# Every product of the last stage with its columns in descending order

## What is computed

```
x = u
# block 1, on LN(x)
z       = rmsnorm(LN(x)) @ in_proj.T            # 768 channels, then a causal 3-tap convolution
x2,x1,v = split(z)
y       = (long_conv(x1*v, h) + x1*v*D) * x2    # h: sums of 16 exponentials per channel
y       = y @ out_proj.T + LN(x)                # out_projection
zm      = rmsnorm(y)
mlp     = gelu(zm @ l1.T) * (zm @ l2.T) @ l3.T  # mlp_block, mlp_down; hidden size 672
x       = x + LN(y + mlp)
# block 2, on LN(x)
W1', W2' = W1, W2 plus rank-one terms from 16 tokens of the batch
hid     = gelu(LN(x) @ W1'.T + b1)              # ffn_up, hidden size 1024
x       = x + LN(hid @ W2'.T + b2)              # ffn_down
```

## Time and profile before

| | us |
|---|---|
| median of 3 runs | 1077.68 |
| lowest, highest | 1077.45, 1081.7 |
| the profiled execution | 1076.75 |
| its span, first to last instruction | 1075.0 |
| TensorE busy in the span | 1050.8 |
| VectorE busy | 877.8 |
| ScalarE busy | 710.8 |
| mean granted TensorE clock | 1.000 |

### The profile page before, as it was taken

One profiled execution on the slowest core, in us unless ns is written; L12 is line 12 of the kernel. 1 busy time (PEld: TensorE's weight loads), 2 busy tenths in 40 slices (PEclk: granted clock), 3 DMA queues, 4 the chain that ended last, 5 costly groups with the idle time before them and its releaser, 6 DMA issues.

```text
span 1075.0 us, 24951 instructions
## 1 busy us (share of the span) xinstructions
PE 1050.8 (98%) x9012; PEld 1008.5 (94%) x9012; DVE 877.8 (82%) x2322; ACT 710.8 (66%) x1589; POOL 299.5 (28%) x575
## 2 busy tenths in 40 slices
PE   8899999999999999999999999999999999999998
PEld 7777888899989999999999999989999999999997
DVE  7999998774788888888887878897888888887776
ACT  7879887764456666666666666656666666666644
POOL 7677775470101112111111111111112111111111
PEclk9999999999999999999999999999999999999999
DMA  3337977986322222233222222432222223222000
GB/s 130 120 117 236 294 216 196 363 318 151 83 66 41 54 57 50 52 52 58 59 60 58 52 51 60 122 96 41 60 51 50 52 53 59 59 58 60 21 21 31
DMA packets 112491, 102.83 MB, mean 96 GB/s; under 512 B 7552, under 2 KB 103744, under 8 KB 112112
## 3 DMA queue, kind: packets, MB, share of 16 engines
q1 hardware_dynamic: 111136, 98.67, 36.2%
q0 software_dynamic: 736, 2.51, 0.6%
q10 hardware_dynamic: 496, 0.05, 0.0%
HBM read 75.75 MB, written 30.70 MB: 99 GB/s over the span
## 4 chain that ended last, share of the span: by engine, by line
PE 67%; DVE 6%; issue 2%; ACT 1%; POOL 0%; POOLq 0%; DVEq 0%; ACTq 0%
PE ps_ring L1551 35%; PE ps_w L1551 16%; PE ps_m L1551 9%; PE ps_o L1551 4%; PE ps_rt L1566 2%; DVE base L1373 1%; PE ps_w L1561 1%; DVE bn L1277 1%; PE ps_m L1617 1%; DVE prod L1320 0%; DVE ht_l L1289 0%; DVE pt_l L1289 0%; POOL sc L1129 0%; ACT rows L1254 0%; DVE yrow L1512 0%
## 5 line engine op out<-in xcount | busy, mean ns | idle before, releaser
L1129 POOL TENSOR_TENSOR sc<-sc,small 128x2 f32<-128x2 f32 x127 | 94.5, 744 | 676.8 <-DVE sc L1501 404.6
L1194 ACT ACTIVATE gate<-ps_ring 128x256 f32<-128x256 f32 x192 | 73.0, 381 | 129.7 <-PE ps_ring L1551 128.9
L1215 ACT ACTIVATE hid<-ps_ring,small 128x256 f32<-128x256 f32 x256 | 112.1, 483 | 24.2 <-PE ps_w L1551 13.4
L1551 PE MATMUL ps_ring<-mt_l,wl_h 128*128 128x256 f32 x640 | 125.5, 277 | 2.6 <-DVE mt_l L1289 2.6
L1551 PE MATMUL ps_ring<-mt_h,wl_h 128*128 128x256 f32 x640 | 125.5, 277 | 1.8 <-DVE prod L1320 1.3
L1551 PE MATMUL ps_ring<-mt_h,wl_l 128*128 128x256 f32 x640 | 124.9, 277 | 0.0
L1289 DVE TENSOR_TENSOR ht_l<-hid,ht_h 128x256 fp32r<-128x256 f32 x256 | 103.1, 423 | 16.5 <-ACT ht_h L1219 10.6
L1551 PE MATMUL ps_ring<-xt_h,we_h 128*128 128x256 f32 x512 | 104.8, 285 | 2.5 <-DVE prod L1320 2.4
L1551 PE MATMUL ps_ring<-xt_h,we_l 128*128 128x256 f32 x512 | 101.3, 279 | 0.0
L1551 PE MATMUL ps_ring<-xt_l,we_h 128*128 128x256 f32 x512 | 101.3, 279 | 0.0
L1320 DVE TENSOR_TENSOR prod<-ps_ring,gate 128x256 f32<-128x256 f32 x192 | 80.7, 420 | 24.2 <-ACT gate L1194 20.6
(11 more groups left out here) (203 smaller groups left out, 2720.2 us busy)
## 6 DMA issues: line engine op xcount, KB each, us to landing
toep_scratch<-taps_scratch SPq DMA_DIRECT2D x26, 512.0 KB, 7.4
toep<-toep_scratch SPq DMA_DIRECT2D x26, 512.0 KB, 8.8
xa<-in_x SPq DMA_DIRECT2D x16, 512.0 KB, 4.9
x_scratch<-x2c SPq DMA_DIRECT2D x16, 512.0 KB, 3.7
x2s<-x_scratch SPq DMA_DIRECT2D x32, 256.0 KB, 6.7
xa_c<-in_x SPq DMA_DIRECT2D x32, 256.0 KB, 2.7
xb_c<-in_x SPq DMA_DIRECT2D x32, 256.0 KB, 2.7
yin<-seq SPq DMA_DIRECT2D x124, 64.0 KB, 5.5
```

Source lines behind the costliest of these rows:

```text
L1129: nc.gpsimd.tensor_tensor(sc[:, to], sc[:, to], neg_half[:, 0, 0:CC], ALU.pow).then_inc(S[done], 1)
L1194: nc.scalar.activation(gate[rows_of, m % 2], ring[m % RING][rows_of, 0], ACT.Gelu_apprx_tanh).then_inc(S["gate_done"], 1)
L1215: nc.scalar.activation(hid[:, m % HIDS], block_of, ACT.Gelu, bias=b1s[:, m:m + 1]).then_inc(S["hid_done"], 1)
L1551: mm = nc.tensor.matmul(out, lhs(a, kk), rhs(b, kk), start=(j == 0), stop=(closed and j == len(todo) - 1))
```

## The change

One line in `product` changes. The last dimension of both the streamed operand and the output is walked from its last element to its first, with step -1. Column 255 of `rhs` goes in first and its result is written to column 255 of `out`, and so on down to column 0. Each result lands in the same element as before, with the same sum. The weights (`lhs`), the count of instructions, their order, the semaphores and every other line are as before. The matmuls at L1561, L1566 and L1617 keep their ascending order.

```
--- before.py
+++ after.py
@@ -1548,7 +1548,7 @@
                     if j == HIGHS_FIRST:
                         for there in highs_ready:
                             pe.wait_ge(*there)
-                    mm = nc.tensor.matmul(out, lhs(a, kk), rhs(b, kk), start=(j == 0),
+                    mm = nc.tensor.matmul(out[:, ::-1], lhs(a, kk), rhs(b, kk)[:, ::-1], start=(j == 0),
                                           stop=(closed and j == len(todo) - 1))
                 return mm
```

## The result

| | before | after |
|---|---|---|
| median, us | 1078.91 (4 runs) | 1101.95 (4 runs) |
| lowest, highest | 1077.45, 1081.7 | 1100.69, 1104.16 |
| ratio, 95% interval | | 1.0213, 1.0184 to 1.0241 |
| the profiled execution | 1076.75 | 1101.98 |
| its span | 1075.0 | 1100.2 |

A forecast was written before the change was run, and what follows sets the result against it. The prediction took the last stage to be bound by distances between matmul starts on a gapless TensorE. Its terms summed 0 + 0 + 0 + 0, giving a median of 1077.7 us, range 1070 to 1102.

The forecast's parts named there:

- rival 2: A small price per matmul, by address phase or the turn at L1617: 1083 to 1101 us, chance 0.20.
- The likeliest case: No change in time: 1077.7 us, own range 1075 to 1081, chance 0.53 within 0.5%.
- What bounds the kernel: Last stage: TensorE without slack, so each ns on the distance between 6528 matmul starts costs 6.5 us.
- Semaphores, weight loads, DMAs, the tail: Parts the change leaves alone, including VectorE, GpSimd and last DMA after the final matmul: 0 us.
- Reading downwards: Streamed operand read with step -1: taken as 0, from a backward VectorE read at the forward rate.
- 119.2 ns, the other end: Upper bound per matmul for reading downwards, if each column takes two slots.
- Writing PSUM downwards: Output written with step -1: taken as 0, bounds 0 or 119.2 ns a matmul, with less confidence.
- half rate: Each descending column takes its own slot, most likely in the PSUM write: 1847 to 1856 us; family's chance 0.20.
- one column in about 120: Share of columns delayed by a slot (0.83 ns of 113) at which the slow side already decides.
- The turn at L1617: 64 places where an add follows a write of the same element: taken as 0, at most 10.4 us.
- Start addresses: Streamed operand starts 1020 bytes further on, beside weight loads: taken as 0, bounds -7.1 to +23.0 us.
- Address phase: one kind of product alone moves: Sign for a price by start address: one product's distance changes, the other kinds keep theirs.

The follow-up runs named there:

- read_only: Step -1 on the streamed operand alone, output written upwards, against the kernel before: 1101.56 us against 1077.59, ratio 1.0226.
- write_only: Step -1 on the output alone, operand streamed upwards, against the kernel before: 1077.83 us, ratio 1.0005.
- down_weights: The change only in output projection, MLP down and second feed-forward product, which stream weight matrices, against the kernel before: 1093.92 us, ratio 1.0163.
- The blocks: Three runs of the kernel before with trains of equal, unread matmuls added at the end, varying operands and order; distances mostly 113.3 to 120.0 ns.
- turn_after: Kernel before, all ascending, with four transposes moved behind the first feed-forward product: 1082.44 us, ratio 1.0053.

## Why the prediction was right and where it wasn't

The range held the time, but by luck: 1101.95 us lies 0.05 under its end of 1102, and 0.95 above the 1083 to 1101 of rival 2, a small price per matmul, which is the case that came. The likeliest case, no change at 1077.7 us with a chance of 0.53, did not come.

- What bounds the kernel: right. From 330 to 560 us TensorE has no gap in either trace, and from 560 to 860 under 4 us of them, so each ns on the distance went straight to the end. 0.84 us more in a unit of 204 matmuls is 4.1 ns each, by 6.5 us per ns some 27 us; 25.2 came, as a few units gained less.
- Semaphores, weight loads, DMAs, the tail: right, 0. The pieces at L1566 and L1617 kept their lengths. (The duration of a matmul of the MLP, which was to stay near 276 ns, became 282.)
- Reading downwards, "I take 0": the step that failed. It took a VectorE row at 1.33 ns a column for a sign about a reader at 0.44 ns, which the text itself called no exclusion. `read_only` measured 24.0 us for it, 3.7 ns a matmul, and 119.2 ns, the other end, was over 30 times too far.
- Writing PSUM downwards, "I take 0": right; `write_only` measured 0.2 us. The half rate named as most likely for this path is shut out on both paths. (That it decides from one column in about 120 is a slip: by the text's own 0.83 of 113 ns it is one in about 136; nothing hangs on it.)
- The turn at L1617: right at 0. The piece is 0.12 us in both traces, where waiting for the drain would have made it 0.28.
- Start addresses: the bound of +23.0 us, made from the kernel's own two distances, was near the right size, and for a related reason: an access order that moves a train from one distance to a slower one. The text took it for a property of the operands ("differ by nothing but the operands"). That was wrong: the same operands stood at 113.3 and 117.8 ns in the kernel before itself, and the ascending MLP moved to 117.7 in `down_weights`. And its arithmetic let the first feed-forward product stay at 117.9 and the rest come up to it; in truth the token products went to 119.8, 1.9 ns above it, and the others to 118. The sum is also too high by its own rows: it takes all the others from 113.3, but rows 3 have 12 matmuls of a unit at 114.2, 15 at 114.7, 24 at 114.2 and 24 at 115.0. With these it is 19.9 us and the top of rival 2 some 1098, so two errors of opposite sign put the end of the range where the time fell.
- "Address phase: one kind of product alone moves" was the sign given to tell it; all kinds moved. The signs for the half rate and the turn were usable and spoke against both.
- The chances: 0.53 for no change was too high. A measured tolerance of 0.83 ns a matmul, two cycles in 272, left hardly any room for "nearly free", and two distances for one shape were already in rows 3.

What stays open: why a train settles at 113.3, 117.8 or 120.0 ns. The blocks show that it depends on the streamed operand's addresses and their order, on where the weights stand to them, and on what ran before; they don't show the mechanism. Traffic of other engines isn't needed for it, since none works beside the blocks. Why the first feed-forward product stands at 117.8 ns in most units and at 113.3 in three of the 28 in the chain is open too. Weights read in the other direction were not tried.

## What to carry to other kernels

On an engine without gaps the price of an edit is its change per instruction times the count, and the page's resolution for "free" is then a fraction of a ns: look for rows of the same shape with different distances before taking 0. Split an edit of two operands into its halves first; here that one comparison settled read against write. Where order doesn't matter, stream the moving operand of a matmul upwards; here a reversal was free on the output, and on the input in halves of 128 columns.

## What the runs showed of the hardware that wasn't expected

- A train of back-to-back matmuls of 256 float32r columns keeps one distance from start to start, here mostly 113.3, 117.8 or 120.0 ns, at a granted clock of 1.00, and what ran before can decide which: in `down_weights` the untouched MLP went from 113.3 to 117.7. The kernel's own operands stood at either of the first two when read upwards, and at one of the last two when read downwards.
- Starting an ascending read two elements in cost as much as reading backwards: 120 ns. Pieces of 16 columns, each descending, cost the most, 133 ns. Each of these was tried once.
- A descending write to PSUM cost nothing: ratio 1.0005.
- Weights taken at every fourth float32 column doubled the distance, to 233 ns.
- Moving four transposes past a product cost 0.5% (`turn_after`), through distances alone.
